# Recurrence output from logistic activations instead of a weighted sum, a denominator and a reciprocal

## The reference, cut to what matters

```python
def step(carry, kv_t):                      # per channel; w = time_decay, u = time_first
    p, q = carry
    k_t, v_t = kv_t
    new_p = maximum(p, u + k_t)
    scale_old = exp(maximum(p - new_p, -30))
    scale_cur = exp(maximum(u + k_t - new_p, -30))
    wkv_t = (scale_old * q + scale_cur * v_t) / (scale_old + scale_cur + 1e-9)
    new_p2 = maximum(p + w, k_t)
    scale_prev = exp(maximum(p + w - new_p2, -30))
    scale_new = exp(maximum(k_t - new_p2, -30))
    q2 = scale_prev * q + scale_new * v_t
    return (new_p2, q2), wkv_t
y = sigmoid(r) * wkv                        # k, v, r: three projections of the mixed input
x = x + y @ W_o.T
h = silu((ln(x) @ w1.T) * s1) * ((ln(x) @ w2.T) * s2)
h = gelu((h @ h1.T) * sh1)
h = gelu((h @ h2.T) * sh2)
x = x + (h @ w3.T) * s3
```

## Time and profile before

| | us |
|---|---|
| median of 3 runs | 1482.34 (1481.42 to 1483.03) |
| span of the profiled execution | 1482.1 |
| PE busy | 1471.7 (99%) |
| PE weight loads busy | 1328.1 (90%) |
| DVE busy | 1204.5 (81%) |
| ACT busy | 1079.5 (73%) |
| POOL busy | 205.5 (14%) |
| distance from one loop round to the next (start of project_out) | 90.37 |

### The profile page before, as it was taken

One profiled execution on the slowest core, in us unless ns is written; L12 is line 12 of the kernel. 1 busy time (PEld: TensorE's weight loads), 2 busy tenths in 40 slices (PEclk: granted clock), 3 DMA queues, 4 the chain that ended last, 5 costly groups with the idle time before them and its releaser, 6 DMA issues.

```text
span 1482.1 us, 28181 instructions
## 1 busy us (share of the span) xinstructions
PE 1471.7 (99%) x10348; PEld 1328.1 (90%) x10348; DVE 1204.5 (81%) x1548; ACT 1079.5 (73%) x1631; POOL 205.5 (14%) x175
## 2 busy tenths in 40 slices
PE   8999999999999999999999999999999999999999
PEld 7989898998989989899898989989899898998998
DVE  7797888868788787887878878688886878878655
ACT  7895776877768676686867768677587776868655
POOL 2313020110201102011030201202011020110200
PEclk9999999999999999999999999999999999999999
DMA  9987574755737467374664746657475673746654
GB/s 353 371 288 257 159 230 109 232 150 184 240 98 242 115 209 221 112 249 117 205 202 139 229 127 211 172 170 232 103 239 134 197 232 97 249 118 204 190 181 135
DMA packets 95070, 285.28 MB, mean 192 GB/s; under 512 B 9152, under 2 KB 33344, under 8 KB 93248
## 3 DMA queue, kind: packets, MB, share of 16 engines
q1 hardware_dynamic: 86880, 277.01, 57.5%
q0 software_dynamic: 8160, 7.87, 4.5%
HBM read 250.76 MB, written 33.03 MB: 191 GB/s over the span
## 4 chain that ended last, share of the span: by engine, by line
PE 91%; DMA 4%; DVE 2%; SPq 1%; issue 1%; POOL 0%; ACT 0%; DVEq 0%; POOLq 0%
PE acc L676 27%; PE acc L678 26%; PE att L569 10%; PE acc L650 7%; PE acc L651 7%; PE acc L702 4%; PE acc L704 4%; PE att L608 3%; DMA stage<-in_w_ffn 2%; PE att L548 2%; DMA scratch<-in_w_ffn 1%; PE att L650 1%; PE att L651 1%; DMA w_plain<-in_w_ffn 1%; DMA spare_slot<-scratch 1%
## 5 line engine op out<-in xcount | busy, mean ns | idle before, releaser
L676 PE MATMUL acc<-op_hi,ring 128*128 128x256 f32 x3360 | 810.8, 286 | 0.5 <-issue 0.5
L678 PE MATMUL acc<-op_lo,ring 128*128 128x256 f32 x3360 | 788.9, 279 | 0.0
L676 PEld LDWEIGHTS acc<-op_hi,ring 128*128 128x128 f32 x3360 | 632.0, 188 | 18.7 <-issue 17.6
L678 PEld LDWEIGHTS acc<-op_lo,ring 128*128 128x128 f32 x3360 | 631.2, 188 | 11.1 <-issue 10.0
L1674 DVE TENSOR_TENSOR op_lo<-blocks,op_hi 128x1024 fp32r<-128x1024 f32 (+2 forms) x271 | 340.7, 1272 | 94.2 <-ACT op_hi L1064 90.5
L1064 ACT ACTIVATE op_hi<-blocks 128x1024 fp32r<-128x1024 f32 (+2 forms) x263 | 283.8, 1091 | 82.8 <-DVE blocks L1669 74.9
L650 PE MATMUL acc<-x_hi,w_rnd 128*128 128x512 f32 x420 | 167.8, 400 | 0.0
L651 PE MATMUL acc<-x_lo,w_rnd 128*128 128x512 f32 x420 | 165.5, 394 | 0.0
L2096 POOL TENSOR_TENSOR v_sb<-mix_v,v_sb 128x1024 f32<-128x1024 f32 (+1 forms) x19 | 39.4, 2071 | 824.0 <-DVE r_sb L1601 817.1
L1104 ACT ACTIVATE blocks<-acc,vec 128x256 f32<-128x256 f32 x268 | 105.2, 476 | 62.4 <-PE acc L678 60.8
L1104 ACT ACTIVATE blocks<-parts,vec 128x256 f32<-128x256 f32 x240 | 102.3, 497 | 56.3 <-DVE parts L1732 48.0
(11 more groups left out here) (212 smaller groups left out, 2106.8 us busy)
## 6 DMA issues: line engine op xcount, KB each, us to landing
ring<-scratch SPq DMA_DIRECT2D x426, 512.0 KB, 4.2
scratch<-stage SPq DMA_DIRECT2D x11, 1024.0 KB, 12.8
stage<-in_w_ffn SPq DMA_DIRECT2D x10, 1024.0 KB, 10.8
x_in<-in_x SPq DMA_DIRECT2D x32, 256.0 KB, 4.6
out<-x_next SPq DMA_DIRECT2D x30, 256.0 KB, 4.9
out<-mix_v POOLq DMA_DIRECT2D x30, 256.0 KB, 4.4
scratch<-in_w_ffn SPq DMA_DIRECT2D x4, 1024.0 KB, 17.5
ring<-stage SPq DMA_DIRECT2D x7, 512.0 KB, 9.2
```

What stands on the lines that cost most here:

```text
L676: pe.matmul(out, act(w), act(op_hi[:, k, c, :]), start=(begins and c == 0 and m % 2 == 0), stop=False, skip_group_check=True)
L678: mm = pe.matmul(out, act(w), act(op_lo[:, k, c, :]), start=False, stop=(c == QC - 1), skip_group_check=True)
```

## The change

Two differences become one: mix_k = k - p (L1534 and L1538 of the changed kernel). Three pairs of per-partition bounds, made once by POOL from decay and first (six operations of 128x2), clamp it three times per chunk. ACT adds decay or first as a per-partition bias, per chunk: Exp for the new and the old weight of the state, and Sigmoid for the two shares of the output, since a / (a + b) is a logistic of the difference. The receptance becomes Sigmoid(r). DVE's sum, product with 1 + exp(-r), reciprocals, and the separate add of the early half go; y is numerator times r in one operation (`gated`). POOL does its three operations on both chunks at once and writes the first into `mix_v`. In `copy_x` ACT waits for y instead of the numerator.

```diff
-            def exp(s, t, k):
-                act.wait_ge(s.dve_pre.sem, s.dve_pre.at(t, (1, 2, 3, 4)[k] if isinstance(t, int) and t < 2 else (3, 4, 1, 2)[k]))
-                ap, sign = ((fresh, -1.0), (norm_ch, 1.0), (mix_v, 1.0), (mix_k, -1.0))[k]
-                s.act_exp.add(act.activation(ap[:, :, s.cols], ap[:, :, s.cols], ACT.Exp, scale=sign))
+            def weight(s, dst, src, func, sign, shift):
+                for c in range(DC):
+                    last_chunk = act.activation(dst[:, c, s.cols], src[:, c, s.cols], func, bias=shift[:, c:c + 1], scale=sign)
+                s.act_exp.add(last_chunk)
+            def exp_new(s, t):
+                act.wait_ge(s.dve_pre.sem, s.dve_pre.at(t, 1))
+                weight(s, fresh, fresh, ACT.Exp, 1.0, minus_decay)
+            def exp_old(s, t):
+                act.wait_ge(s.dve_pre.sem, s.dve_pre.at(t, 2))
+                weight(s, norm_ch, norm_ch, ACT.Exp, -1.0, decay)
+            def share_new(s, t):
+                act.wait_ge(s.dve_pre.sem, s.dve_pre.at(t, 3))
+                act.wait_ge(s.pe_kvr.sem, s.pe_kvr.at(t, 2 * DC))
+                weight(s, mix_v, mix_k, ACT.Sigmoid, 1.0, first)
+            def share_old(s, t):
+                weight(s, mix_k, mix_k, ACT.Sigmoid, -1.0, minus_first)
...
-                s.act_exp.add(act.activation(r_sb[:, :, s.cols], r_sb[:, :, s.cols], ACT.Exp, scale=-1.0))
+                s.act_exp.add(act.activation(r_sb[:, :, s.cols], r_sb[:, :, s.cols], ACT.Sigmoid))
...
+            def distance(s, t):
+                dve.wait_ge(s.pe_kvr.sem, s.pe_kvr.at(t, DC))
+                if s is WHOLE:
+                    link(s, dve.tensor_tensor(by_seq(mix_k[:]), by_seq(k_sb[:]), before, ALU.subtract))
+                    return
...
+            def clamp(s, dst, low, high):
                 for c in range(DC):
+                    last_chunk = dve.tensor_scalar(dst[:, c, s.cols], mix_k[:, c, s.cols], low[:, c:c + 1], high[:, c:c + 1], ALU.max, ALU.min)
+                s.dve_pre.add(last_chunk)
...
-            for c in range(DC):
-                invert(late_seq, 0, [c])
-                weigh_first(late_seq, c)
+            mixed_first(late_seq)
...
-                invert(WHOLE, t)
                 c12(i, 1)
-                weigh(WHOLE, t)
+                gated(WHOLE, t)
...
+                pool.wait_ge(s.act_exp.sem, s.act_exp.at(t, 5 if s is FIRST[1] else 4))
+                v_, old_q = mix_v[:, :, s.cols], by_seq(norm_ch)[:, :, s.seqs]
+                s.pool_chain.link(pool.tensor_tensor(v_, v_, v_sb[:, :, s.cols], ALU.mult))
                 pool.wait_ge(s.dve_q.sem, s.dve_q.at(t))
+                s.pool_chain.link(pool.tensor_tensor(old_q, by_seq(mix_k[:])[:, :, s.seqs], before[:, :, s.seqs], ALU.mult))
+                settle(s, t)
+                s.pool_num.add(pool.tensor_tensor(fresh[:, :, s.cols], v_, norm_ch[:, :, s.cols], ALU.add))
```

More of the change, by code:

```diff
@@ L33 @@
 LN_EPS = 1e-5
-WKV_EPS = 1e-9
 WARM = (16, 5, 2, 1, 2)
@@ L215, in build @@
         zeros = sb("zeros", [P, NB])
+        bounds = sb("bounds", [P, 6 * DC])
         low_sums = sb("low_sums", [P, sum(CHECKS)])
@@ L275, in build @@
         s1, s2, sh1, sh2 = (vec[:, 5 * DC + HC * j:5 * DC + HC * (j + 1)] for j in range(4))
+        now_floor, now_top, minus_first, new_floor, old_top, minus_decay = (bounds[:, DC * j:DC * (j + 1)] for j in range(6))
         norm_ch = norm[:].rearrange("p (c t) -> p c t", c=DC)
@@ L1227, in _ @@
             copy_late_x()
-            exp(early_seq, 0, 0)
-            exp(early_seq, 0, 1)
+            act.wait_ge(setup_bounds, 6)
+            exp_new(early_seq, 0)
+            exp_old(early_seq, 0)
             copy_kvr(early_seq, 0, range(2, 3 * DC))
-            exp(early_seq, 0, 2)
-            exp(early_seq, 0, 3)
-            exp_r(early_seq, 0)
+            share_new(early_seq, 0)
+            share_old(early_seq, 0)
+            receptance(early_seq, 0)
             seed_x(early_seq, 0)
@@ L1245, in _ @@
             copy_kvr(late_seq, 0, range(2 * DC, 3 * DC))
[L1246 to L1250, removed]
+            exp_new(late_seq, 0)
+            exp_old(late_seq, 0)
+            share_new(late_seq, 0)
+            share_old(late_seq, 0)
+            receptance(late_seq, 0)
             for m in range(4):
@@ L1295, in _ @@
             gelu_plain(0, 1, 1)
-            for k in range(4):
-                exp(WHOLE, 1, k)
+            exp_new(WHOLE, 1)
+            exp_old(WHOLE, 1)
+            share_new(WHOLE, 1)
+            share_old(WHOLE, 1)
             copy_kvr(WHOLE, 1, [4, 5])
-            exp_r(WHOLE, 1)
+            receptance(WHOLE, 1)
             seed_x(WHOLE, 1)
@@ L1355, in _ @@
                 hiT23(i)
-                exp(WHOLE, i + 1, 3)
+                share_new(WHOLE, i + 1)
                 p1(i, 1)
                 hiB21(i)
+                share_old(WHOLE, i + 1)
                 copy_kvr(WHOLE, i + 1, [5])
-                exp_r(WHOLE, i + 1)
+                receptance(WHOLE, i + 1)
                 p5(i, 1)
@@ L1621, in weigh_first, with mixed_first @@
                     s.dve_y.add(y)
-            def weigh(s, t):
-                dve.wait_ge(s.pool_num.sem, s.pool_num.at(t))
-                settle(s, t)
-                s.dve_y.add(dve.tensor_tensor(v_sb[:, :, s.cols], fresh[:, :, s.cols], k_sb[:, :, s.cols], ALU.mult))
+            def mixed_first(s):
+                for c in range(DC):
+                    gated(s, 0, slice(c, c + 1))
             def ln2_statistics(s, t):
@@ L1887, in _ @@
             prod_first(0, 7)
-            denominator(late_seq, 0)
             lo_first(0, 1, 0)
-            gated_denominator(late_seq, 0)
             lo_first(0, 1, 1)
-            for c in range(DC):
-                invert(late_seq, 0, [c])
-                weigh_first(late_seq, c)
+            mixed_first(late_seq)
             set_flag(1)
```

129 lines of the change are left out of this document (27 added, 102 removed).

## The result

| | before | changed |
|---|---|---|
| median of 4 runs, us | 1481.91 (1481.42 to 1483.03) | 1488.34 (1487.85 to 1488.89) |
| ratio to before, 95% interval | | 1.0043 (1.0029 to 1.0057) |
| span of the profiled execution | 1482.1 | 1486.9 |

The changed kernel is slower by 6.4 us. The prediction was 1486.7, with a range of 1483.0 to 1489.2. The time lies in the range and on the side that was forecast, 1.6 above the forecast itself. But the two profiled spans are only 4.8 apart, and the sum was +4.4, so 2 us have to be explained. They turn out to be two gains in the sum that a usual execution of the kernel before does not offer, and a loss that was priced only as a rival.

The account below looks back on a forecast made before the run. PE was taken to bound the kernel, with losses and gains only in straight code before the loop. Terms 2.05 + 3.1 - 0.2 - 0.8 + 1.2 - 0.9 = +4.4 on span 1482.1, plus 0.24 to the median: 1486.7 us, range 1483.0 to 1489.2.

Parts of the forecast that it names:

- Prices on ACT: Two biased halves take 0.81 for 0.52 in tile 0, 1.24 for 0.955 later; a table load 1.28, with lost overlap 1.4.
- Loop: 0: The loop costs nothing: `p5` ends at 200.5, PE needs it at 201.70, so 1.2 us of room.
- Early half: +2.05: Tile 0: held clamp, wider pairs and a table load make ACT late; PE starts its gate 2.05 us later.
- Late half: +3.1 and -0.2: Tile 0: ACT 4.0 later ahead of the first Silu, PE waits 3.1 us; its 0.2 wait for late y goes.
- (e): PE's clock falls to 1.2 GHz in its added late-half waits: +1.6, 1488.3; no chance of its own, inside the forecast's range.
- Second gate: -0.8: PE's 0.8 us wait for `blocks` ends, because `x_in` is there by the time the later DVE needs it.
- Tile 1: +1.2: Straight code: halved Exps and one load delay the Gelu that frees PE's bank; PE loses 1.2 us.
- Last norm: -0.9: Before the loop: DVE is several microseconds earlier, so PE's 0.9 us wait for `norm` ends.
- (a): ACT's added work in the start is covered, only gains stay: -2.7, 1479.6; 5%, and 22% in part.
- (b): Loop: work ahead of `p5` exceeds its room by 0.3, PE waits 14 times: 4.2 more, 1490.9; 4%.
- (c): A change of tables takes a second 1.28 each time; four added ones cost 5.1, 1491.8; 2%.
- (d): The loop gets faster with 10 us less DVE work in each round: about 1478; 3%.

Follow-up runs that it names:

- start_both: Changed kernel, in tiles 0 and 1 Exp in place of Sigmoid and unbiased activations of both chunks at once: 1481.69 us.
- loop_room: Changed kernel with one unused Gelu ahead of the old share in each of the 14 loop rounds, forcing two more table loads: 1519.57 us.
- warm_two: Changed kernel with two unused matmuls ahead of PE's wait for chunk 7 of the first gate: 1487.83 us.
- both_orders: Changed kernel with tile 0's late shares behind the Silu results and tile 1's bank-freeing Gelu ahead of one sum of low bits: 1486.71 us.
- start_whole: Changed kernel, in tiles 0 and 1 each biased pair made one unbiased activation of both chunks, table loads kept: 1485.97 us.
- start_exp: Changed kernel with Exp in place of Sigmoid in tiles 0 and 1, leaving out four table loads: 1484.82 us.

## Why the prediction was right, point by point

- **The bound.** Right: PE never waits in the loop, and its start sets everything. DVE's relief is worth nothing (start_both).
- **Prices on ACT.** Right: a biased pair of 256 columns goes on after 0.81 (36.97 to 37.78; forecast 0.81), of 512 after 1.25 (99.28 to 100.53; 1.24), a load 1.28. The clamps on DVE were not priced: a pair of 256 columns with pointers goes on after 0.65 (32.44 to 33.09) where one of 512 with constants did after 0.46 (30.58 to 31.04). It is the second instruction that costs, not the pointers: of 512 columns a pair with pointers goes on after 0.92 (94.25 to 95.17), 0.46 for each. DVE's room covered it.
- **Loop: 0.** Right. `p5` ends at 205.5 in a round that starts 5.07 later, so at 200.4 (forecast 200.5).

```profile
204.48 1.01 ACT L1101 ACTIVATE parts<-acc 128x1024 f32<-128x1024 f32 x1
```

- **Early half: +2.05.** Right, 2.0, though PE meets it in waits ahead of the gate and not at the gate.
- **Late half: +3.1 and -0.2.** ACT's part is 3.3. The 0.2 of the late y came back as a wait of 0.2 behind it. Missing in the sum was the clock: 0.8. It stood as rival (e) with 1.6, so it was in the range.
- **Second gate: -0.8.** Wrong. The step took a wait of one profiled execution for a property of the kernel. It came from `x_in`, which had landed late in that one. Nor did the transfer stand still, as the step says: in the changed kernel it is issued 2.0 later (50.1 against 48.1), and DVE doesn't wait for it.
- **Tile 1: +1.2.** Right, 1.27.
- **Last norm: -0.9.** Wrong in the same way. In the second profile of before DVE's last rest takes 1.22, where the first had 2.06, and DVE as a whole is earlier, so the deviation comes in time. What held the operation in the first isn't shown. First and second profile of before:

```profile
124.73 2.06 DVE L1674 TENSOR_TENSOR op_lo<-blocks,op_hi 128x1024 fp32r<-128x1024 f32 x1
```

```profile
123.07 1.22 DVE L1674 TENSOR_TENSOR op_lo<-blocks,op_hi 128x1024 fp32r<-128x1024 f32 x1
```

- **From the sum to the median.** Wrong: the 0.24 compared the span of a long execution with the median of others. A time lies 1.7 above its own span. The profiled span was 2.0 above the median span of 1480.1. That the two errors mostly cancelled is luck: 1480.1 + 1.7 + 4.4 would have been 1486.2. The low end of the range has a slip too: with the 0.2 of the late y in it the cheap sum is +0.6 and not +0.8.
- **Rivals.** (a) is out: the cover on ACT doesn't hold, and there were no gains. (b) didn't happen; its room was 1.0 as loop_room shows. (c) is out by the 2.80 of loop_room, (d) by the unchanged 90.37. (e) happened with half of its price, and not in every execution.

So the mechanism, ACT's work ahead of the first Silu and of tile 1's Gelu, and its prices were right, and the forecast was too low by the two gains and the clock. The sum between the profiled executions is 2.0 + 3.3 + 0.8 + 1.3 = 7.4, where the forecast had 4.4. That the time still lies in the range is owed to the width that was given to the price of the bias, which came out as it was taken.

## What to carry to other kernels

Before a wait is booked as a gain, ask what ended last ahead of it: if that was a transfer or an operation that another engine held up, it may be missing in the next execution, and a second profile of the same kernel tells. A function that needs another table costs its load on the path wherever the engine has no idle time up to the next place where it is waited for; another order can win a part back (2.4 of 4.15 here), and the rest comes up at the next such place. Work that was taken from an engine with spare time, 158 us of it here, was worth nothing.

## What the runs showed of the hardware

- The granted clock can fall for 3.4 us behind a wait of PE, and not in every execution nor behind every such wait: behind the 2.0 in both profiles of the changed kernel; at the first gate in warm_two, both_orders and start_whole (in warm_two groups of four matmuls are 0.85 apart from 35.95 to 39.35 and 0.47 after), but not in the changed kernel; and behind three of the fourteen waits of 1.8 in loop_room. Each in the loop costs 1.6 to 1.7. Where another engine sets the time anyway, it costs nothing.
- Matmuls of 512 columns of f32 without rounding take 0.86 us each, as two entries of 0.43.
- From the last DVE instruction to the end of the span, with the last output transfers in it, pass 2.1 us in the changed kernel (1484.77 to 1486.9), 4.3 us in start_exp (1478.90 to 1483.2) and 3.6 in start_whole, with the same instructions; in all other profiles 2.1 to 2.3.
